# Attention scores of a head pair as two row tiles of 49 rows and 64 columns, with the maxima unit in 64-row tiles beside them

## The reference, cut to what matters

```python
qh = split_heads(layernorm(x) @ Wq.T)          # (8, 16, 64, 16), the second layer adds biases
kh = split_heads(ctx_1024 @ Wk.T)              # (8, 16, 1601, 16)
vh = split_heads(ctx_1024 @ Wv.T)
attn = softmax(einsum('bhqd,bhkd->bhqk', qh, kh) / sqrt(16))
x = x + merge_heads(einsum('bhqk,bhkd->bhqd', attn, vh)) @ Wo.T
```

## Time and profile before

| | |
|---|---|
| median of 3 runs | 1107.54 us |
| the profiled execution | 1111.19 us, span 1109.4 us |
| mean granted TensorE clock | 0.959 of full speed |
| busy: PE, PEld, DVE, ACT, POOL | 91%, 60%, 58%, 51%, 13% |
| scores of round 0 start | 48.30 us |
| scores of round 9, 10, 11 start | 482.49, 530.12, 576.00 us |
| last scores start | 780.9 us |
| DMAs issued by SP | 646, of which 384 restack keys and 96 load queries |

### The profile page before, as it was taken

The page is one execution under the profiler, slowest core; times in us unless marked ns, Lnnn a source line. Parts: engine busy times, 40 slices in busy tenths (PEclk is TensorE's granted clock), DMA queues, the critical chain, the costliest instruction groups (busy, mean ns, idle before and its releaser), DMA issues.

```text
span 1109.4 us, 31381 instructions
## 1 busy us (share of the span) xinstructions
PE 1014.5 (91%) x13428; PEld 662.1 (60%) x13428; DVE 642.5 (58%) x1063; ACT 563.2 (51%) x1012; POOL 148.0 (13%) x180
## 2 busy tenths in 40 slices
PE   5788899999999999999899999999648999999998
PEld 2466567666756666676666666666425444445887
DVE  5675655756565466666657657664457454436342
ACT  4587666665675655456465565556237222222210
POOL 3211111111111111111111121110000000000000
PEclk9999899998999999999999999998559999999999
DMA  7785556453544343443434334422201222222210
GB/s 234 212 257 164 158 142 180 99 152 82 158 137 122 71 127 73 113 109 87 122 88 112 85 98 112 94 77 91 76 1 38 76 90 101 96 95 86 105 39 20
DMA packets 71894, 121.47 MB, mean 109 GB/s; under 512 B 34775, under 2 KB 48247, under 8 KB 68555
## 3 DMA queue, kind: packets, MB, share of 16 engines
q1 hardware_dynamic: 70924, 117.79, 37.3%
q0 software_dynamic: 544, 1.34, 0.3%
q10 hardware_dynamic: 288, 0.33, 0.1%
HBM read 63.82 MB, written 16.26 MB: 72 GB/s over the span
## 4 chain that ended last, share of the span: by engine, by line
PE 76%; DVE 12%; ACT 4%; issue 3%; DMA 2%; SPq 2%; POOL 0%; ACTq 0%; DVEq 0%
PE ps L590 74%; DVE mpart L1173 3%; SPq L377 2%; PE ps L835 1%; DVE rinv L1190 1%; DMA c32b<-in_ctxT 1%; ACT p L954 1%; PE ps L720 1%; ACT kh L932 1%; DVE cl L1148 1%; ACT ch L915 1%; DVE oT L1193 1%; DMA stage<-in_fw 1%; DVE st L1117 1%; DMA qscratch<-qbl 0%
## 5 line engine op out<-in xcount | busy, mean ns | idle before, releaser
L1173 DVE TENSOR_REDUCE mpart<-ps 128x2 f32<-128x800 f32 (+1 forms) x256 | 253.2, 990 | 145.1 <-PE ps L590 143.8
L954 ACT ACTIVATE p<-ps 128x512 f32<-128x512 f32 (+1 forms) x416 | 225.3, 595 | 120.3 <-PE ps L590 118.2
L544 POOL TENSOR_TENSOR kl<-k,kh 128x400 f16<-128x400 f32 (+1 forms) x128 | 117.2, 916 | 512.5 <-ACT kh L932 504.4
L590 PE MATMUL ps<-p,v 128*17 128x64 f32 x6656 | 138.1, 226 | 0.6 <-DVE osum L1200 0.6
L590 PE MATMUL ps<-qcur,ks 97*128 97x128 f16 (+1 forms) x1664 | 134.0, 223 | 4.9 <-ACT p L954 2.2
L1204 DVE SCALAR_TENSOR_TENSOR wl<-w,wh 128x2048 f16<-128x2048 f32 x24 | 55.0, 2292 | 126.1 <-ACT wh L965 126.1
L590 PEld LDWEIGHTS ps<-p,v 128*17 128x17 f32 x6656 | 101.6, 100 | 40.0 <-issue 31.0
L590 PEld LDWEIGHTS ps<-qcur,ks 97*128 97x128 f16 (+1 forms) x1664 | 103.9, 101 | 31.6 <-issue 9.7
L590 PE MATMUL ps<-wvh,ch 128*128 128x256 f16 (+1 forms) x416 | 114.8, 276 | 4.6 <-ACT kh L932 3.6
L590 PE MATMUL ps<-wvh,cl 128*128 128x256 f16 (+1 forms) x416 | 113.9, 274 | 0.0
L590 PE MATMUL ps<-wvl,ch 128*128 128x256 f16 (+1 forms) x416 | 113.9, 274 | 0.0
(11 more groups left out here) (205 smaller groups left out, 1431.8 us busy)
## 6 DMA issues: line engine op xcount, KB each, us to landing
ks<-kh SPq DMA_DIRECT2D x256, 100.1 KB
w<-in_wgu SPq DMA_DIRECT2D x16, 1024.0 KB, 4.8
ks<-kl SPq DMA_DIRECT2D x128, 100.1 KB
w<-in_wd SPq DMA_DIRECT2D x8, 1024.0 KB, 4.8
c32a<-in_ctxT SPq DMA_DIRECT2D x16, 400.5 KB, 4.7
cparts<-ch SPq DMA_DIRECT2D x8, 800.5 KB, 6.3
cparts<-cl SPq DMA_DIRECT2D x8, 800.5 KB, 7.5
c32a<-in_ctxT SPq DMA_DIRECT2D x12, 400.0 KB, 3.5
```

The source lines that it names most:

```text
L544: nc.gpsimd.tensor_tensor(kl[:, mt, k0:k0 + w], k32[:, ku % 2, 0:w], kh[:, mt, k0:k0 + w], ALU.subtract).then_inc(sem("klo_done"), 1)
L590: return nc.tensor.matmul(o, lhsT, rhs, start=start, stop=stop, skip_group_check=shared)
L954: nc.scalar.activation(p32[0:n, step % PRING, BANK * hb:BANK * hb + BANK], ps[0:n, hb, :], ACT.Exp, scale=DH ** -0.5).then_inc(sem("exp_do ...
L1173: nc.vector.reduce_max(mpart[:, j0:j0 + 2, quarter], o.rearrange("p (b c) -> p b c", b=2)[:, :, 0:w], AX.X).then_inc(sem("max_done"), 1)
```

## The change

The two heads of a pair no longer share one matmul. Head A's 49 rows (a row of ones, 16 rows of high keys, 16 of low keys, 16 of high keys) lie in partitions 0 to 48, head B's in partitions 64 to 112. S is now 16 matmuls of 64 columns, two for each pair, the one in the upper and the other in the lower 64 rows of the array, and they write two banks: all A heads to bank 0, all B heads to bank 1. Both banks are finished only at the end of S, so S waits for both exponentials of the step before. `weigh` finds the heads of `p32` in the new places.

`restack` copies 16 partitions at a time, 24 DMAs for each call. `load_queries` issues 12 DMAs of 16 partitions, `load_high_queries` 4 of 32 partitions. `qbcur` has two versions of each query tile, with the rows of the other pair zero (cleared once by POOL at the start), so that a P unit can contract over 64 partitions; a P unit takes pairs 2 apart. The row of the maxima is written by two ACT instructions. In the prologue DVE makes `qbcur[0]` by four copies instead of one, and the ones are loaded by four DMAs instead of two. In steps 0 to 11, S moves from the front of the step to just ahead of the step's last P unit.

```diff
-STACK = 96
+SIDE = 64
+STACK = 3 * DH + 1
...
-              2: ["S", "V4", "P3", "W"],
+              2: ["V4", "S", "P3", "W"],
...
-              6: ["S", "P7", "K6", "P8", "W"],
+              6: ["P7", "K6", "S", "P8", "W"],
...
-    return (2 * (i // 4), i % 4) if i < NP else (NP // 2 + 2 * (i % 2), (i - NP) // 2)
+    return (i // 4, i % 4) if i < NP else (NP // 2 + i % 2, (i - NP) // 2)
...
                 for j in range(4):
-                    rr, pair = slice(32 * j, 32 * j + 32), 4 * mt + j
-                    load(ks[r % 2][0:32, pair, :], kh[rr, mt, :], f"stacked{mt}")
-                    load(ks[r % 2][32:64, pair, :], kl[rr, mt, :], f"stacked{mt}")
-                    load(ks[r % 2][64:96, pair, :], kh[rr, mt, :], f"stacked{mt}")
+                    for side in range(2):
+                        head = slice(32 * j + DH * side, 32 * j + DH * side + DH)
+                        for n, part in enumerate((kh, kl, kh)):
+                            row = SIDE * side + 1 + DH * n
+                            load(ks[r % 2][row:row + DH, 4 * mt + j, :], part[head, mt, :], f"stacked{mt}")
...
-                for row, part in ((0, 0), (32, 0), (64, 1)):
+                for n, part in enumerate((0, 0, 1)):
                     for mt in range(2):
-                        load(qcur[r % 2][row:row + 32, 4 * mt:4 * mt + 4, :],
-                             d["qscratch"][layer, part, :, mt, b, :].rearrange("(j r) c -> r j c", j=4), "qcur_in")
+                        for side in range(2):
+                            row = SIDE * side + 1 + DH * n
+                            heads = d["qscratch"][layer, part, :, mt, b, NQ * side:NQ * side + NQ]
+                            load(qcur[r % 2][row:row + DH, 4 * mt:4 * mt + 4, :],
+                                 heads.rearrange("(j s r) c -> s r j c", j=4, s=2)[side], "qcur_in")
...
-                load(qbcur[r % 2][:, :, :], d["qscratch"][layer, 0, :, :, b, :], f"qbcur_in{r % 2}")
+                for j in range(4):
+                    rr = slice(32 * j, 32 * j + 32)
+                    load(qbcur[r % 2][rr, :, j % 2, :], d["qscratch"][layer, 0, rr, :, b, :], f"qbcur_in{r % 2}")
...
             nc.gpsimd.memset(half[:, :], -0.5).then_inc(sem("half_ready"), 1)
+            nc.gpsimd.memset(qbcur[0][:, :, :, :], 0.0)
+            nc.gpsimd.memset(qbcur[1][:, :, :, :], 0.0).then_inc(sem("qb_zero"), 1)
...
-                    rr = slice(32 * (j0 % 4 + n), 32 * (j0 % 4 + n) + 32)
-                    last = mm(o[:, BANK * n:BANK * n + w], qbcur[r % 2][rr, mt, :], kh[rr, mt, k0:k0 + w], True, True)
+                    rr = slice(SIDE * n, SIDE * n + SIDE)
+                    last = mm(o[:, BANK * n:BANK * n + w], qbcur[r % 2][rr, mt, j0 % 2, :], kh[rr, mt, k0:k0 + w], True,
+                              True)
...
-                for hb in range(2):
-                    need(pe, "exp_done", 2 * KT * g + 2 * k - 1 + hb)
-                    for jj in range(4):
-                        j = 4 * hb + jj
-                        last = mm(ps[0:n, hb, P * jj:P * jj + P], ks[u][0:STACK + 1, j, P * k:P * k + n], qcur[u][:, j, :],
+                need(pe, "exp_done", 2 * KT * g + 2 * k)
+                for j in range(NP):
+                    for side in range(2):
+                        rr = slice(SIDE * side, SIDE * side + STACK)
+                        last = mm(ps[0:n, side, NQ * j:NQ * j + NQ], ks[u][rr, j, P * k:P * k + n], qcur[u][rr, j, :],
                                   True, True)
```

More of the change, by code:

```diff
@@ L353, in build @@
         p32 = sb(ctx, "p32", [P, PRING, H * NQ])
-        qcur = [sb(ctx, f"qcur{i}", [STACK + 1, NP, P], F16) for i in range(2)]
-        qbcur = [sb(ctx, f"qbcur{i}", [P, 2, P], F16) for i in range(2)]
+        qcur = [sb(ctx, f"qcur{i}", [P, NP, NQ], F16) for i in range(2)]
+        qbcur = [sb(ctx, f"qbcur{i}", [P, 2, 2, P], F16) for i in range(2)]
         mpart = sb(ctx, "mpart", [P, NP, 4])
@@ L464, in _ @@
                 load_ctx(n)
-            load(ks[0][STACK:STACK + 1, :, :], d["ones"], "ones_in")
-            load(ks[1][STACK:STACK + 1, :, :], d["ones"], "ones_in")
+            for u in range(2):
+                for side in range(2):
+                    load(ks[u][SIDE * side:SIDE * side + 1, :, :], d["ones"], "ones_in")
             store_queries(0, 0)
@@ L677, in scores @@
                 if k == 0:
-                    pe.wait_ge(sem("qcur_in"), 16 * 6 * (g + 1))
+                    pe.wait_ge(sem("qcur_in"), 16 * 12 * (g + 1))
                     pe.wait_ge(sem("row_done"), g + 1)
                     for mt in range(2):
-                        pe.wait_ge(sem(f"stacked{mt}"), 16 * 12 * (g + 1))
-                for hb in range(2):
-                    need(pe, "exp_done", 2 * KT * g + 2 * k - 1 + hb)
-                    for jj in range(4):
-                        j = 4 * hb + jj
-                        last = mm(ps[0:n, hb, P * jj:P * jj + P], ks[u][0:STACK + 1, j, P * k:P * k + n], qcur[u][:, j, :],
+                        pe.wait_ge(sem(f"stacked{mt}"), 16 * 24 * (g + 1))
+                need(pe, "exp_done", 2 * KT * g + 2 * k)
+                for j in range(NP):
+                    for side in range(2):
+                        rr = slice(SIDE * side, SIDE * side + STACK)
+                        last = mm(ps[0:n, side, NQ * j:NQ * j + NQ], ks[u][rr, j, P * k:P * k + n], qcur[u][rr, j, :],
                                   True, True)
-                    last.then_inc(sem("main_mm"), 1)
+                        if j == NP - 1:
+                            last.then_inc(sem("main_mm"), 1)
             def weigh(g, k):
@@ L700, in weigh @@
                         h = 4 * gr + c
-                        last = mm(pvb[32 * c:32 * c + VW, gr, :], v[0:n, k, h, :], p32[0:n, buf, NQ * h:NQ * h + NQ],
+                        at = BANK * (h % 2) + NQ * (h // 2)
+                        last = mm(pvb[32 * c:32 * c + VW, gr, :], v[0:n, k, h, :], p32[0:n, buf, at:at + NQ],
                                   k == 0 and gr == 0, k == KT - 1, True)
@@ L943, in after_unit @@
                     need(act, "main_mm", 2 * KT * (r - 1))
-                    nc.scalar.activation(qcur[r % 2][STACK:STACK + 1, :, :],
-                                         o[0:1, :].rearrange("p (j q) -> p j q", j=NP), ACT.Copy, scale=-1.0)\
-                       .then_inc(sem("row_done"), 1)
+                    for side in range(2):
+                        ins = nc.scalar.activation(qcur[r % 2][SIDE * side:SIDE * side + 1, :, :],
+                                                   o[0:1, :].rearrange("p (j s q) -> p s j q", j=NP, s=2)[:, side],
+                                                   ACT.Copy, scale=-1.0)
+                    ins.then_inc(sem("row_done"), 1)
             def exps(g, k):
@@ L951, in exps @@
                 need(act, "pv_mm", step - PRING + 1)
-                for hb in range(2):
-                    act.wait_ge(sem("main_mm"), 2 * step + hb + 1)
-                    nc.scalar.activation(p32[0:n, step % PRING, BANK * hb:BANK * hb + BANK], ps[0:n, hb, :],
+                for side in range(2):
+                    act.wait_ge(sem("main_mm"), 2 * step + side + 1)
+                    nc.scalar.activation(p32[0:n, step % PRING, BANK * side:BANK * side + BANK], ps[0:n, side, :],
                                          ACT.Exp, scale=DH ** -0.5).then_inc(sem("exp_done"), 1)
@@ L1370, in _ @@
             dve.wait_ge(sem("qb_ready"), 1)
-            nc.vector.tensor_copy(qbcur[0][:, :, :].rearrange("p m (h q) -> p m h q", h=2), qbh[:, :, 0, :, :])\
-              .then_inc(sem("qbcur_first"), 1)
+            dve.wait_ge(sem("qb_zero"), 1)
+            for j in range(4):
+                rr = slice(32 * j, 32 * j + 32)
+                ins = nc.vector.tensor_copy(qbcur[0][rr, :, j % 2, :].rearrange("p m (h q) -> p m h q", h=2),
+                                            qbh[rr, :, 0, :, :])
+            ins.then_inc(sem("qbcur_first"), 1)
             split_ctx(2)
```

30 lines of the change are left out of this document (16 added, 14 removed).

## The result

| | kernel before | changed kernel |
|---|---|---|
| time, median | 1107.78 us (1107.4 to 1109.19) | 1209.58 us (1208.4 to 1212.64) |
| ratio | | 1.092, interval 1.090 to 1.094 |
| profiled execution, its span | 1111.2, 1109.4 | 1210.0, 1208.2 |
| mean granted clock of TensorE | 0.959 | 0.914 |
| first S of round 0 / of round 1 / of round 15 | 48.3 / 90.3 / 751.6 | 71.6 / 124.9 / 846.1 |

The change makes the kernel 9% slower: 102 us, three times the +33 forecast, and outside the range of 1096 to 1172.

A forecast was written before the change was run, and what follows sets the result against it. PE was taken to bound the kernel, busy 91% of the span, so its savings count in full. Against 1111.2 us: -32 + 21 + 6 + 14 + 24 = +33, 1144, or 1140.5 from the median; forecast 1140, range 1096 to 1172.

The forecast's parts named there:

- SP's issues: start: Prologue: SP issues 76 DMAs where 37 stood, so round 0's S starts at 68.1 instead of 48.30; 21 us lost.
- round 0: wait for the keys of round 1: Round 1's second restack has even less time than those of rounds 11 to 15; 6 us lost.
- rounds, waits for keys: Rounds 11 to 15: the second restack and the four P loads behind it come late; 14 us lost.
- rounds, waits for `a_w`: Rounds 3, 5, 7 and 9: the `a_w` load lands near 488, PE arrives at 481.6; 6 us each, 24 us.
- tiles and order: PE's shorter S and fewer tiling changes, less the waits from moving S ahead of P: 32 us gained.
- the step "P": First P units of steps 1, 6, 11 wait for DVE, 1.2 a round, 0.2 in step 6; PE still gains 2.0 a round.
- S's 0.22: Each step's S takes 0.23 us instead of 0.45 in two row tiles; 0.22 saved over 208 steps, 46 us.
- fewer changes of tiling: S beside P drops one 0.10 us change of the array's split in steps 0, 1, 6, 11, 12; 8 us gained.
- Rival 4: S waits on ACT's late exponentials in steps with K, losing 20 us of the gain: 1155 us; chance 0.08.
- rival 3: SP saturated throughout: 49 us of issuing in rounds of 46.8, deciding from 0.70 an issue: 1170 us; chance 0.13.
- cheap small issues: 16-partition issues under about 0.45 us give 1084, at 0.50 to 0.55 1095 to 1105; chance 0.22 for the two.
- The rule weighed there: About 60 cycles, 25 ns, a matmul make S 0.40: a gain of 0.05 a step, 10 us in all.

The follow-up runs named there:

- e1: Changed kernel with the old number of SP issues (12 key copies, 6 query loads, 1 P load; values not the reference's): 1106.02 us, 0.998.
- e4: Kernel before with only the changed kernel's new order of units, S ahead of P: 1129.68 us, 1.018.
- e5: Changed kernel with the old number of issues and the old order, so the tiles alone (values not the reference's): 1099.85 us, 0.994.
- e14: Row tiles in the old order, with head B's key copies and 18 query copies of the first two rounds issued by GpSimd: 1100.06 us, 0.994.
- e2: Kernel before with doubled issues, from 646 to 1171, in old tiles and old order: 1208.09 us, 1.089.
- e8: Changed kernel with 12 filler matmuls of 512 columns ahead of each round's first scores: 1214.61 us, 1.096, mean clock 0.926 instead of 0.914.
- e6: Kernel before with only the issues ahead of round 0 doubled: 1134.31 us, 1.026, first scores at 70.0 us instead of 48.3.
- e7: Changed kernel with the old order of units and head B's key copies issued by GpSimd instead of SP: 1112.92 us, 1.004.
- e3: Changed kernel with the old order of units, S at the front of a step: 1208.25 us, 1.089.
- e13: Row tiles, old order, head B's key copies on GpSimd, SP's loads ahead of round 0 reordered, round 1's high query copies before the second restack: 1112.73 us, 1.003.

## Why the prediction was wrong

The direction and the mechanism of the loss were right: SP's queue takes the lead and PE waits for keys, queries and `a_w`. The sum failed, +33 for +102. The changed kernel against e1, the same kernel with the old issues, splits its span without a rest: start 71.6 - 50.3 = 21.3, round 0 53.3 - 43.4 = 9.9, rounds 1 to 14 721.2 - 651.1 = 70.1, all later 2.7; together 104.0 = 1208.2 - 1104.2.

| term | forecast | measured |
|---|---|---|
| SP's issues: start | +21 | +21 |
| round 0: wait for the keys of round 1 | +6 | +5 |
| round 0: PE longer busy (clock 0.85 for 0.96), rest | none | +5 |
| rounds, waits for keys and, nearly all of the rest, P's queries | +14 | +34 (17.1 + 16.7) |
| rounds, waits for `a_w` | +24 | +17 |
| rounds, PE at the lower clock | none | +19 |
| tail | none | +3 |
| tiles and order (e1 against before) | -32 | -2 by medians, -5 by spans |

**The gain on PE (the step "P" with its 2.0 a round, 32 us) failed most, by 27 to 30 us.** Its pieces were sized well: S to P 0.24 for 0.23, and the wait that the order adds before P is 22 us in e4, for 1.4 a round forecast. What failed is that the sum took the rest of S's saved time as time of the kernel and put PE's other waits at nothing. Windows over rounds 1 to 14 of the kernel before, then of e1 (us, busy us and instructions of each engine, granted clock, DMA share, GB/s), and two of e1's waits in them:
```profile
90.30:751.60 661.30, 628.08 (x10260) 424.30 (x10259) 415.45 (x719) 401.18 (x777) 110.54 (x130) 0.97 0.44 115
```
```profile
93.70:744.80 651.10, 588.16 (x11717) 383.45 (x11716) 408.57 (x719) 396.17 (x791) 112.19 (x130) 0.97 0.44 115
```
```profile
PE ps L598 <- DVE mpart L1186: 39.1, 39, 4.2
PE ps L598 <- DVE osum L1213: 5.7, 10, 1.0
```
PE is 39.9 us less busy, as much as S's 0.22 in 14 x 13 steps alone; the sum had 7 more here for fewer changes of tiling. It is 29.7 us more idle. 20.2 of these are waits for DVE's reduction (18.9 before), as forecast; 9.5 are further idle time that the sum did not have, among it waits for DVE's `osum` (5.7 for 0.6) and for ScalarE's exponentials (3.1 for 0.2). So the rounds gained 10.2 where 28 (14 x 2.0) were forecast, and start, round 0 and tail lost 5 together.

With the old order (e5) some 18 of PE's 35 us go into waits as well. One step of e14's timeline shows how; in the kernel before P began 551.03 - 548.62 = 2.41 after S:
```profile
550.16 0.41 PE L631 MATMUL ps<-qcur,ks 49*128 49x64 f16 x16
552.58 0.34 PE L631 MATMUL ps<-kh,qbcur 64*128 64x400 f16 x2 [2.01 <-DVE mpart L1223]
```
It is 2.42 still; the wait grew from 1.79 to 2.01, by just what S saved. This one step the forecast had seen and priced; the others it had not. The 91% of busy time in the earlier trace rows and the 3.3 us of idle before S in the earlier trace rows did not mean that PE alone was the bound: part of its work ran in step with DVE's reductions and ScalarE's exponentials. How much of the missing gain each of the further waits holds, and why start, round 0 and tail lost 5 us, stays open. Rival 4 named the exponentials; its place was right, and its 20 us were 12.6 in e5.

**Waits in the rounds.** The forecast made 38 us, the trace has 51. The 16.0 us of waits for keys in the list above hold the one of round 1, which belongs to round 0, and lack that of round 15 (5.7 us, ahead of 846.15), which gives 17.1:
```profile
124.95 0.61 PE L603 MATMUL ps<-qcur,ks 49*128 49x64 f16 x16 [4.57 <-DMA ks<-kh]
```
Round 9 came as worked out (the `a_w` load 8.6 us behind the copies, 8.8 forecast; wait 4.7, 6 forecast). What was missed: key copies take 0.74 each there, (545.87 - 528.00) / 24, not 0.68, and keys come late in rounds 5, 7 and 9 too, P's queries (14.3 of the 16.7 us) in ten rounds, not in 1 and 11 to 15. SP saturated throughout, rival 3, was the case, with more than 0.70 an issue as its condition said. It gave a round 49 us; they took 721.2 / 14 = 51.5.

**The clock** had no term. The same window of the changed kernel:
```profile
124.90:846.10 721.20, 607.14 (x11716) 393.11 (x11716) 409.50 (x719) 395.41 (x789) 111.43 (x129) 0.93 0.44 103
```
The same matmuls as in e1 are busy 19 us longer, at a granted clock of 0.93 for 0.97; in e2, with the old tiles, it is 19 us too against the kernel before (647.5 to 628.1, 0.94 for 0.97). With the waits, 51 us, that is the 70 of the rounds. That the lower clock costs this on the path is only argued; e8 raised the clock but put its own work in the way, so no run shows what the clock alone would give back.

**Issue price, start.** 0.60 was near (0.66), and the start's 21 us are what e6 shows too. The doubt that I priced at 0.22, cheap small issues, had nothing in it.

The rule weighed there, a fixed overhead of about 60 cycles for each matmul (the Trainium skill, "TensorEngine Tiling (Array Packing)", section Performance Considerations), would by the prediction's estimate have made S 0.40; the trace disagrees, 16 matmuls in 0.24 us, 15 ns each, including the way to P.

On e7 and e14 the Trainium skill ("Trainium Kernel Development and Optimization", section Key Constraints) says that DMAs from several queues run on the same engines, and that a second queue saves only the issue time. The runs agree, and here the issue time was what bound: 108 of e3's 1208 us came back in e14, whose key copies are as many and as small as the changed kernel's.

## What to carry to other kernels

Where a layout doubles the number of DMAs, count them against the slack of the queue that issues them (here SP's waits for keys ready, 172 us in fourteen rounds, 12 a round, against 15 to 18 us of further key issues, 24 at 0.63 to 0.74), and look for a queue that stands idle before giving the layout up. A change that shortens one engine's work is worth its time only where that engine isn't in step with others: move the start of the shortened unit in the timeline and ask what the next waiting unit waits for. Here PE also lost clock when it began to wait (0.97 to 0.93 in the rounds), and that belongs in the sum.

## What the runs showed of the hardware

- Issuing an SBUF to SBUF copy of 3202 bytes a row costs SP 0.589 us for 16 partitions and 0.594 for 32 at the median, 0.63 from start to start, 0.74 on average in round 9; GpSimd's issue of the same copy costs 0.487, and beside it SP's median stayed 0.590 (e14).
- Two 49-row tiles of 64 columns run side by side: 16 matmuls and the way to P in 0.24 us, where 8 of 128 columns took 0.45. A change between split and whole array costs about 0.10 us: 0.20 from the last V matmul to S, where V matmuls start 0.11 apart.
- While the DMA engines were busy all the time (327 GB/s from 56 to 70 us in e13) query copies of 8 KB took SP up to 2.2 us each to issue, for 0.43 at the median in the changed kernel.
